# A graph layer with experts on one core: the item list of the preparation stage made in its last turns

## What is computed

```python
edge_index = jnp.stack([src, dst])                 # 200000 edges, sorted by dst; 6250 nodes, 256 features
xn = _layernorm(x, axis=-1)
x = x + _L0_gnn_ref(edge_index, xn, W, b) + _L0_mix_ref(xn[None], ...)[0]
x = x + _L0_ffn_ref(_layernorm(x, axis=-1)[None], ...)[0]
...
# _L0_gnn_ref: graph convolution with self loops
deg = jax.ops.segment_sum(jnp.ones_like(dst, dtype=X.dtype), dst, num_segments=N)
dinv = jnp.where(deg > 0, jax.lax.rsqrt(deg), 0.0)
norm = dinv[src] * dinv[dst]
h = X @ W
msgs = h[src] * norm[:, None]
out = jax.ops.segment_sum(msgs, dst, num_segments=N) + b
```

## The kernel before

| step | TensorE, and its turn before | what it waits for | VectorE behind it |
|---|---|---|---|
| histogram | L722, 13 matmuls, turn 3 | `keyed` | L452 `hist` |
| totals | L729, turn 6 | L452 | L456 `totals` |
| counts and chunks | L734, L735, turn 9 | L456 | L461 to L464, `item_chunk`, `item_dst` |
| spread and places | L743, turn 12 | L464 | L468 to L479, `item_block`, `place_in` |

## Time and profile before

### The profile page before, as it was taken

The page is one execution under the profiler, slowest core; times in us unless marked ns, Lnnn a source line. Parts: engine busy times, 40 slices in busy tenths (PEclk is TensorE's granted clock), DMA queues, the critical chain, the costliest instruction groups (busy, mean ns, idle before and its releaser), DMA issues. The chain is left out here.

```text
span 2453.0 us, 41210 instructions
## 1 busy us (share of the span) xinstructions
PE 2157.4 (88%) x13789; PEld 1545.6 (63%) x13789; DVE 1770.2 (72%) x5676; ACT 1213.4 (49%) x2731; POOL 366.4 (15%) x396
## 2 busy tenths in 40 slices
PE   3739999998998999888899899999989995999997
PEld 2625655566666666666666666666656654999897
DVE  3564544478887888888888888866766754887886
ACT  0435544455555555555555555444444444655563
POOL 7100000001111111111111011100000002333432
PEclk7869999999999999999999999999999997999999
DMA  5000000000000000000000000000010004222220
GB/s 182 13 7 3 3 3 3 3 3 5 3 3 3 5 3 3 3 5 3 3 3 3 3 5 3 6 29 29 31 38 29 29 27 124 79 68 87 88 81 9
DMA packets 52135, 63.54 MB, mean 26 GB/s; under 512 B 15695, under 2 KB 44330, under 8 KB 51808
## 3 DMA queue, kind: packets, MB, share of 16 engines
q1 hardware_dynamic: 27104, 29.06, 3.7%
q0 software_dynamic: 10336, 21.41, 3.2%
q10 hardware_dynamic: 14496, 10.53, 1.3%
HBM read 42.82 MB, written 20.92 MB: 26 GB/s over the span
## 5 line engine op out<-in xcount | busy, mean ns | idle before, releaser
L1189 PE MATMUL p_m<-node_halves,adj 128*128 128x512 f16 x3626 | 986.5, 389 | 17.1 <-DVE rows_v L1813 14.2
L1574 ACT CAST adj<-p_b 128x392 f16<-128x392 f32 x1184 | 570.0, 485 | 843.0 <-PE p_b L1179 827.7
L1786 DVE TENSOR_TENSOR one_src<-iota,codes 128x512 bf16<-128x512 bf16 x1184 | 503.8, 425 | 428.7 <-PE p_b L1179 418.8
L1179 PE MATMUL p_b<-one_edge,one_src 128*128 128x98 bf16 x4736 | 613.3, 266 | 54.8 <-ACT adj L1574 39.6
L1179 PEld LDWEIGHTS p_b<-one_edge,one_src 128*128 128x128 bf16 x4736 | 458.3, 116 | 298.9 <-DVE one_src L1786 61.9
L1189 PEld LDWEIGHTS p_m<-node_halves,adj 128*128 128x128 f16 x3626 | 360.1, 105 | 246.5 <-issue 41.4
L1786 DVE TENSOR_TENSOR one_edge<-iota,codes 128x392 bf16<-128x392 bf16 x1184 | 429.0, 362 | 0.0
L1103 POOL TENSOR_TENSOR x1r<-x1n,bc_ln1g 128x256 f32<-128x256 f32 x49 | 44.9, 916 | 840.1 <-ACT x1n L1498 840.1
L1092 POOL DMA_INDIRECT src_e<-in_srcR,item_chunk x37 | 38.2, 1033 | 727.8 <-DVEq L1808 726.3
L1156 POOL DMA_INDIRECT out_dram<-oo,slot_node x64 | 74.8, 1168 | 219.7 <-DVE oo L2210 203.1
L1138 POOL DMA_INDIRECT rows<-node_features,slot_row x64 | 73.2, 1144 | 165.7 <-DVE slot_node L2317 146.6
(11 more groups left out here) (343 smaller groups left out, 3530.9 us busy)
## 6 DMA issues: line engine op xcount, KB each, us to landing
w1raw<-in_w SPq DMA_DIRECT2D x8, 1024.0 KB, 5.3
w2raw<-in_w SPq DMA_DIRECT2D x8, 1024.0 KB
res<-in_x SPq DMA_DIRECT2D x7, 896.0 KB, 7.5
node_features<-res ACTq DMA_DIRECT2D x20, 256.0 KB
out_dram<-res ACTq DMA_DIRECT2D x20, 256.0 KB
out_dram<-res SPq DMA_DIRECT2D x1, 1152.0 KB
fb_b<-in_fb SPq DMA_DIRECT2D x1, 1024.0 KB, 9.2
rows<-node_features,slot_row POOLq DMA_INDIRECT x64, 4.9
```

What stands on the lines that cost most here:

```text
L1179: mm = pe.matmul(p_b[n % 2][:, u * HI2:(u + 1) * HI2], one_src[:, n % ONER, :, u], one_edge[:, n % ONER, :, u], start=True, stop=True)
L1189: mm = pe.matmul(p_m[:], adj[:, k % 2, h, :], node16[:, h, :], start=(h == 0), stop=(h == NBLK - 1))
L1574: nc.scalar.copy(adj[:, n // SPV % 2, :, n % SPV * 2 * IB:(n % SPV + 1) * 2 * IB] .rearrange("p h (u r) -> p h u r", r=2), p_b[n % 2][:, 0 ...
L1786: V.tensor_tensor(tile[:, n % ONER], iota4[:, 0:m, :], codes[:, q % 2, a, at:at + IB].rearrange("p (m u) -> p m u", m=1) .broadcast_to([P, ...
```

## The change

All four steps of the item list are moved, on TensorE and on VectorE. Nothing is added or left out. On TensorE the histogram stands in turn 24, the totals in turn 25, the counts in turn 26, and the spread behind the loop, ahead of `shift(2)`. On VectorE the reading of the histogram stands ahead of `inverse_degrees(1)`, that of the totals ahead of `scaled_rows(1)`, the chunks behind `scaled_rows(1)` and the places behind `positions(5)`.

```diff
@@ -193,7 +193,7 @@
-    HIST_AT, TOTALS_AT, COUNTS_AT, SPREAD_AT = 3, 6, 9, 12
+    HIST_AT, TOTALS_AT, COUNTS_AT = 24, 25, 26
@@ -560,18 +560,12 @@
-            statistics(0)
-            statistics(1)
-            item_histogram()
-            statistics(2)
-            item_totals()
-            statistics(3)
+            for gi in range(4):
+                statistics(gi)
             inverse_std(0)
             positions(0)
-            item_chunks()
             for gi in range(4, NG):
                 statistics(gi)
-            item_places()
             positions(1)
@@ -582,9 +576,13 @@
             positions(3)
             degrees(1)
             positions(4)
+            item_histogram()
             inverse_degrees(1)
+            item_totals()
             scaled_rows(1)
+            item_chunks()
             positions(5)
+            item_places()
             degrees(2)
             low_halves(1)
@@ -753,8 +751,6 @@
-                if t == SPREAD_AT:
-                    item_spread()
@@ -762,6 +758,7 @@
                 if t == 0:
                     column_sums()
+            item_spread()
             shift(2)
             shift(3)
```

## The result

| | before | changed |
|---|---|---|
| median, lowest, highest of 20 runs each, us | 2458.65, 2455.13, 2465.30 | 2462.19, 2459.85, 2466.59 |
| ratio to before, with its 95% interval | | 1.0015 [1.0008, 1.0022] |
| the profiled execution's own time and span, us | 2454.8, 2453.0 | 2462.28, 2460.5 |
| first instruction of the second block, us | 159.93 | 163.37 |
| last VectorE instruction of `prepare` starts, us | 159.00 | 162.45 |

The changed kernel is 3.5 us slower by the medians, inside the 0.2% that I called hard to tell from no change. The preparation ends 3.45 us later (162.45 - 159.00), and that is the whole difference: the two spans differ by 7.5 us, but 4.0 of them lie in the second block (2460.5 - 163.37 = 2297.1 against 2453.0 - 159.93 = 2293.1), whose code is unchanged. In eight later traces on two chips that rest is 2294.0 to 2297.1 in six, and 2303.8 and 2304.2 in two.

The account below looks back on a forecast made before the run.

Parts of the forecast that it names:

- The standstill: Early stretch of the preparation where TensorE, VectorE and ScalarE mostly stand; its end was taken as unchanged, 81.7 us.
- Rival B: The standstill begins with the histogram's matmuls and shrinks without them: 2452.4 us, or 2410 with none left; chance 0.24.
- rival A: TensorE leaves the standstill one turn further on, worth 2.16 us, all kept: 2460.8 us; chance 0.16.
- The first shift: TensorE up to turn 15, without counts, spread and a wait: 2.0 us earlier, 103.9 instead of 105.88.
- VectorE, positions(1): VectorE from 82 to 103 us, rid of early list work: `positions(1)` starts at 96.2 instead of 103.15.
- The histogram's wait: VectorE ahead of `inverse_degrees(1)` waits about 1.7 us for turn 24; the 2.0 us won are given back but for 0.4.
- Rival C: TensorE stays at 1.2 GHz through turns 22 to 24; histogram and totals 3.3 us later: +7.6, 2466.3 us; chance 0.13.
- The totals' wait: VectorE ahead of `scaled_rows(1)` waits 0.9 us for turn 25's totals; the scaling starts 0.9 us later than before.
- Chunks and places: On VectorE behind the second group's scaling, without a gap: 0.65 and 2.77 us, +3.4 in full on the path.
- Counts and spread: TensorE's counts (0.6 us) lie beside `scaled_rows(1)`, its spread (0.98 us) beside `positions(5)`; counts hidden, spread covered.
- The remark on the second wait: Part of VectorE's early gain could be kept with nothing put behind its second wait; bounded by 0.4 and 2.0 us.
- gaps: Follow-up theory: without a standstill, late list work on VectorE replaces early work on the path; ratio 0.9995 to 1.0000.

Follow-up runs that it names:

- the last experiment: Against the changed kernel: histogram, totals, counts, spread in turns 6, 14, 18, 22, VectorE's list steps put at its waits for ScalarE; 2457.74 us against 2462.33.

## Why the prediction was right

The end was forecast at +4.3 us and is +3.45 by the trace and +3.5 by the medians: 2463.0 predicted, 2462.19 measured, "within 0.2%" the likeliest. By its steps:

- *The standstill.* "I take its end, 81.7 us, as it is": 81.76. Rival B is out: the standstill begins without any histogram, so it is not the histogram's. But **the step was incomplete**: the extra turn of rival A, to which I gave 0.16, was there. A's time, 2460.8, already counts the waits for histogram and totals; what kept the result above it is the lower clock behind the second shift (1.1 us), and the first shift, 3.70 earlier and not 4.2.
- *The first shift*, forecast 2.0 us earlier within 1.4 and 4.2: 3.70, by the turn. This is the term that was mis-sized.
- *VectorE, positions(1)* at 96.2: 95.34.
- *The histogram's wait*, forecast 1.7: 4.27. Part of this is a slip in my working: 129.6, from which I counted the wait, is when VectorE was free before (131.91 less 2.33), and less the 2.0 us won it is 127.6, so the text should have said 3.7. It had no effect, since the copy's start was worked out from TensorE: 131.3 forecast, 130.59 measured. The mechanism, a gain given back at this wait, is the one that the text names.
- *Rival C*, TensorE at 1.2 GHz behind the second shift: not through turns 23 and 24 (1.89 us for turn 23's products), but the low level was there from the shift's first matmul on and lasted into turn 23's transposes, and the way from shift to turn 24 is 1.1 us longer. That is a third of the 3.3 us that C named, and the forecast had none of it.
- *The totals' wait*, forecast 0.9: 1.14; the scaling forecast 0.9 later: 0.10. The difference of 0.8 does not arise at this wait, which was longer than forecast. It comes from above: TensorE reached turn 24 0.5 us before the time forecast (130.07 against 130.6), 1.7 by the first shift less 1.1 by the clock, and VectorE had the histogram 0.2 sooner behind it. It makes nearly the whole difference between 4.3 and 3.45.
- *Luck.* So the close number rests on two terms that were missing and nearly cancel, the turn and the clock. Without the lower clock the same rows would give some +2.3, an estimate (3.35 + 0.10 - 1.13). And 0.85 us is less than the 1.8 by which four traces of the same code differ at this point.
- *Chunks and places*, +3.4, in full on the path: +3.35, and the doubled places confirm the price with +2.62 for 2.4. Counts and spread are hidden, as forecast: VectorE goes from `positions(5)` through the places to `low_halves(1)` at 142.59 with no wait.
- *The remark on the second wait*, that part of the gain could be kept if nothing were put behind it, is borne out by the last experiment: its second inverse degrees stand 2.2 us ahead of the first trace of the kernel before (129.67 against 131.91), with the places ahead of them. The remark's words are wrong in one thing: the 2.18 and 2.33 us are VectorE's waits for ScalarE's roots of two groups, not a root's for TensorE.

One reading of the page was loose: the first slice is not the weakest of all, the third shows the same 3 tenths. The sum does not use it.

What the prediction could not see: the profile's tens of us of "remote" waits were absent in all four traces of chip 4. Why the counts come late in one place and not in the other stays open. So does the change's exact effect without a standstill: the changed kernel itself was never timed on chip 4, where "gaps" expected no loss and its nearest relative, with the histogram in turn 3, began the second block 0.7 us late.

By the record TensorE's turn 4 ended at 30.3 us in the changed kernel (28.38 + 1.89), and its count was seen at 71.15. The Trainium skill ("Perfetto Trace Analysis", Tensor Engine Instruction) holds that a matmul's end in a profile is estimated and the count rises when PSUM acknowledges; the trace agrees that the recorded end is no sign of when the count is seen: here 41 us lie between them.

## What to carry to other kernels

Work moved out of the way of an early chain is worth what the next wait leaves of it: look where the two engines meet next, and expect little if the same work is waited for there. Put side work on an engine into a gap where it waits for another one's short answer (here 2.3 to 2.8 us for the second root), not behind the last of them, where here each us was paid. When two kernels differ by 3 us, ask how far one of them differs from itself: here the same code reached one point at times 1.8 us apart. And where a profile shows counts seen tens of us late, compare with a second chip before building on it.

## What the runs showed of the hardware

While the standstill lasts, counts are seen only at rare moments and instructions start on a grid. VectorE's statistics 3 in the changed kernel's repeat:

```profile
52.38 0.18 DVE L491 BATCH_NORM_AGGREGATE mv<-stats 128x2 f32<-128x6 f32 x1 [1.22 <-remote]
53.78 0.18 DVE L491 BATCH_NORM_AGGREGATE mv<-stats 128x2 f32<-128x6 f32 x1 [1.22 <-remote]
```

They start 1.40 us apart, one pair 0.70 (50.28 and 50.98), though each takes 0.18. In the last experiment the histogram's matmuls of turn 6 fall into it, with no wait between them in the code. Nine of the thirteen start one behind the other from 41.79 on, the last three stand so:

```profile
45.48 0.19 PE L721 MATMUL p_item_list<-one_hi,one_lo 128*128 128x37 bf16 x1 [2.63 <-issue]
48.27 0.19 PE L721 MATMUL p_item_list<-one_hi,one_lo 128*128 128x37 bf16 x1 [2.60 <-issue]
51.08 0.19 PE L721 MATMUL p_item_list<-one_hi,one_lo 128*128 128x37 bf16 x1 [2.62 <-issue]
```

2.8 us apart, four steps of the same 0.70. Later, the single products of turn 6 start at 74.17, 76.28, 79.07, 80.47 and 81.89, three, four, two and two such steps apart. So not only counts are seen late, plain matmuls in a row go at this pace too. The slowing meets TensorE, VectorE and ScalarE, goes with the stretch of GpSimd's transfers (shown on chip 9 by moving it) and is absent in the traces of chip 4; GpSimd's own transfers are issued every 1.25 us all the while. What it is the runs don't show.
